# Attention passes of a graph network: bf16 one-hots and their transposes two halves ahead, evicted ahead of the exponential

## The reference, cut to what matters

```python
msg = feat @ W
scores = leaky_relu((msg @ a[:dh])[src] + (msg @ a[dh:])[dst], 0.2)
e = exp(scores - scores.max())
denom = segment_sum(e, dst)
out = segment_sum(msg[src] * (e / denom[dst])[:, None], dst)
```

## Time and profile before

| what | value |
|---|---|
| median of 3 runs | 7888.87 us (7878.3 to 7893.55) |
| span of the profiled execution | 7890.3 us, 195306 instructions |
| its own device time | not listed apart from the span; the span is 1.4 us above the median |
| TensorE matmuls busy | 5464.8 us (69%) |
| VectorE busy | 4825.2 us (61%) |
| ScalarE busy | 3085.2 us (39%) |
| GpSimd busy | 5124.5 us (65%) |
| mean granted TensorE clock | 0.709 |

### The profile page before, as it was taken

How to read it: one execution, slowest core, us unless ns; L and a number is a source line. 1 busy time by engine, 2 the same in 40 slices (tenths; PEclk the granted TensorE clock), 3 DMA queues, 4 the chain that set the end, 5 groups by cost and what they waited for, 6 DMA issues and landing times.

```text
span 7890.3 us, 195306 instructions
## 1 busy us (share of the span) xinstructions
PE 5464.8 (69%) x50500; PEld 3952.8 (50%) x50501; DVE 4825.2 (61%) x14588; ACT 3085.2 (39%) x7615; POOL 5124.5 (65%) x4726
## 2 busy tenths in 40 slices
PE   3767677777773746777776777435878874888887
PEld 3655556565651336666666666323444442444444
DVE  7555555555556556666666666575666663555555
ACT  2111111111121135555555555413555552666665
POOL 1776767676740157777777777025887784777777
PEclk9977675656555855555555555567999996999999
DMA  3223232323233532222222222033555553544444
GB/s 122 57 56 77 56 77 56 77 56 77 56 76 125 148 47 52 52 51 51 51 51 51 51 51 51 12 91 95 124 124 125 124 125 92 120 116 118 118 118 107
DMA packets 600102, 647.29 MB, mean 82 GB/s; under 512 B 331121, under 2 KB 490355, under 8 KB 599665
## 3 DMA queue, kind: packets, MB, share of 16 engines
q0 software_dynamic: 190000, 384.58, 23.9%
q1 hardware_dynamic: 338379, 238.04, 10.4%
q10 hardware_dynamic: 71640, 23.81, 1.2%
HBM read 562.39 MB, written 83.23 MB: 82 GB/s over the span
## 4 chain that ended last, share of the span: by engine, by line
DVE 27%; issue 19%; POOL 15%; DMA 14%; PE 13%; DVEq 5%; ACT 3%; SPq 3%; ACTq 1%; POOLq 0%
POOL acc L659 8%; POOL rows L639 7%; DMA acc<-list_dst 7%; PE psa L1407 4%; PE psc L1366 3%; DMA rows<-t_gat,idx 2%; DVE acc L1729 2%; DVE acc L1781 1%; DMA acc<-in_x 1%; DVEq L619 1%; DMA acc<-y_d 1%; DVE acc L1728 1%; ACT ohb L1120 1%; PE psc L1498 1%; DVE s_m L1837 1%
## 5 line engine op out<-in xcount | busy, mean ns | idle before, releaser
L639 POOL DMA_INDIRECT rows<-t_gat,idx x3168 | 3142.8, 992 | 1189.8 <-issue 903.3
L659 POOL DMA_INDIRECT acc<-t_part,acc x1400 | 1826.6, 1305 | 546.6 <-issue 460.2
L1407 PE MATMUL psa<-rhs,rows 128*128 128x176 f32 (+1 forms) x6336 | 1713.1, 431 | 23.2 <-DVEq L1922 12.2
L1217 ACT ACTIVATE acc<-psa 128x384 bf16<-128x384 f32 x3200 | 1290.2, 506 | 884.7 <-PE psa L1481 765.8
L1407 PEld LDWEIGHTS psa<-rhs,rows 128*128 128x128 f32 x6336 | 1497.2, 311 | 132.0 <-DVEq L1922 83.2
L1481 PE MATMUL psa<-den,rhs 125*32 125x384 bf16 x12800 | 785.2, 343 | 191.4 <-ACT acc L1217 149.8
L1128 ACT ACTIVATE wgt<-s_d 128x64 f32<-128x64 f32 (+1 forms) x396 | 93.8, 237 | 1625.5 <-DVE s_d L1838 1610.8
L1122 ACT ACTIVATE oht<-psc 22x1024 bf16<-22x1024 bf16 x402 | 407.3, 1013 | 783.9 <-PE psc L1366 730.4
L1395 PE MATMUL psc<-oh,wgt 128*8 128x22 f32 (+1 forms) x6336 | 290.2, 205 | 552.1 <-ACT wgt L1128 543.8
L1071 ACT ACTIVATE acc<-stg,acc 128x128 bf16<-128x128 f32 x1818 | 552.9, 387 | 198.2 <-issue 116.0
L1481 PEld LDWEIGHTS psa<-den,rhs 125*32 125x32 bf16 x12800 | 285.6, 97 | 641.9 <-ACT acc L1217 412.7
(11 more groups left out here) (348 smaller groups left out, 7870.4 us busy)
## 6 DMA issues: line engine op xcount, KB each, us to landing
rows<-list_src SPq DMA_DIRECT2D x200, 500.0 KB
rows<-t_gat,idx POOLq DMA_INDIRECT x3168
acc<-y_d SPq DMA_DIRECT2D x50, 1000.0 KB, 5.0
y_d<-stg SPq DMA_DIRECT2D x100, 250.0 KB, 2.8
acc<-t_part,acc POOLq DMA_INDIRECT x1400
acc<-t_sage SPq DMA_DIRECT2D x300, 62.5 KB
adw<-win_d SPq DMA_DIRECT2D x820, 2.2 KB
adw<-win_d SPq DMA_DIRECT2D x788, 0.4 KB
```

What stands on the lines that cost most here:

```text
L639: eng.indirect_dma_start(rows[:, j, 0:spec["width"]], None, spec["table"], bass.IndirectOffsetOnAxis(ap=idx[:, j:j + 1], axis=0)).then_inc ...
L659: eng.indirect_dma_start(h_prow[u][:, t, :], None, t_parts[layer], bass.IndirectOffsetOnAxis(ap=h_idx[u][:, t:t + 1], axis=0)).then_inc(h_ ...
L1217: eng.activation(h_rows[:, g, :], psa[:, g % 4, 0:D3], ACT.Copy).then_inc(hyb["ev"], 1)
L1407: last = eng.matmul(sums(half, q, h), rows[:, slot * TH + j, 0:D], right, start=(j == 2 * q), stop=(j == 2 * q + 1))
```

## The change

It applies to the weighted passes G0 and G1.
- A new order `two_ahead` on TensorE and VectorE: `early` runs two halves ahead, `late` one half ahead. For TensorE `early` is the transposes and `late` the scores; for VectorE `early` is `cur`, `rel` and `ohb`, and `late` is `oh`.
- In G1 VectorE makes `ohb` itself, from `rel_all`; ScalarE's copy L1120 is gone.
- On TensorE the denominators of m are followed at once by pairs 0 and 1; then come the scores of m+1, the transposes of m+2, and pairs 2 and 3.
- On ScalarE `oht` of m+1 is evicted ahead of the exponential of m, and the list work follows the exponential at once.
- `rel` has two buffers. At the end of each run ScalarE evicts once more and TensorE waits for it and increments `adx_ready`; the counters of SP, TensorE and VectorE are moved to suit.

```diff
+        def two_ahead(eng, spec, lo, hi, nxt, early, late, main):
+            slots = spec["slots"]
+            early(lo, 0, True)
+            late(lo, 0, True)
+            early(lo, 1, False)
+            with eng.Fori(lo, hi, spec["step"]) as b:
+                for slot in range(slots - 2):
+                    main(b, slot, lambda: late(b, slot + 1, False), lambda: early(b, slot + 2, False))
+                ahead = next_trip(eng, spec, nxt, b)
+                main(b, slots - 2, lambda: late(b, slots - 1, False), lambda: early(ahead, 0, False))
+                main(b, slots - 1, lambda: late(ahead, 0, False), lambda: early(ahead, 1, False))
...
@@ ScalarE: act_pass
-            def front(b, slot, first):
-                half = slot % 2
+            def evict_oht(b, slot, first):
                 f = count(eng, nf, MAX_HALVES)
-                if h == 1:
-                    eng.wait_ge(oh_ready, f)
-                    eng.activation(ohb[:, half, :, :], oh[:, half, :, :], ACT.Copy).then_inc(ohb_ready, 1)
                 eng.wait_ge(oht_ps, f)
                 eng.activation(oht[:, :, :], p_oht[0:WIN, :, 0:EP], ACT.Copy).then_inc(oht_sb, 1)
+            def run(s0, v, lo, hi, w0):
+                halves(eng, spec, lo, hi, nxt, evict_oht, main)
+                evict_oht(hi, 1, False)
...
                 m = count(eng, nm, MAX_HALVES)
+                next_oht()
                 eng.wait_ge(exp_arg, m)
                 eng.activation(wgt[:, half, :, 0:h], s_d[:, :, 0:h], ACT.Exp).then_inc(wgt_ready, 1)
-                next_front()
@@ TensorE: pe_pass, main and run
-                next_front()
+                if not spec["weighted"]:
+                    next_scores()
                 for q in range(PAIRS):
                     if q == PAIRS // 2 and spec["weighted"]:
-                        scores(1 - half)
+                        next_scores()
+                        next_transposes()
...
+                two_ahead(eng, spec, lo, hi, nxt, transposes, scores_of, main)
+                eng.wait_ge(oht_sb, value(eng, nf))
+                eng.sem_inc(adx_ready, 1)
@@ VectorE: dve_pass
+                def late(b, slot, first):
+                    eng.tensor_tensor(oh[:, slot % 2, :, :], iota_w[:, :].unsqueeze(1).to_broadcast([EP, TH, WIN]),
+                                      rel_of(b, slot).unsqueeze(2).to_broadcast([EP, TH, WIN]),
+                                      ALU.is_equal).then_inc(oh_ready, 1)
+                def early(b, slot, first):
...
+                    if not lists:
+                        shifts(b, slot, link)
+                    if weighted:
+                        eng.tensor_tensor(ohb[:, half, :, :], iota_w[:, :].unsqueeze(1).to_broadcast([EP, TH, WIN]),
+                                          rel_of(b, slot).unsqueeze(2).to_broadcast([EP, TH, WIN]),
+                                          ALU.is_equal).then_inc(ohb_ready, 1)
+                    link.end()
...
-                        eng.wait_ge(adx_ready, value(eng, nf) + 2)
+                        eng.wait_ge(adx_ready, value(eng, nf) + 1)
...
-                    next_front()
+                    next_late()
+                    next_early()
```

More of the change, by code:

```diff
@@ L215, in gnn_kernel @@
         cur = sb("cur", [EP, PAIRS])
-        rel = sb("rel", [EP, TH])
+        rel = sb("rel", [EP, 2, TH])
         oh = sb("oh", [EP, 2, TH, WIN])
@@ L866, in run @@
                 halves(eng, spec, lo, hi, nxt[0], front, main)
+                if spec["weighted"]:
+                    eng.reg_add(nf, nf, 1)
             def after(s):
@@ L1113, in act_pass, with main @@
                 squares, evict, store_idx, counted = act_lists(eng, lists)
-            def front(b, slot, first):
-                half = slot % 2
+            def evict_oht(b, slot, first):
                 f = count(eng, nf, MAX_HALVES)
-                if h == 1:
-                    eng.wait_ge(oh_ready, f)
-                    eng.activation(ohb[:, half, :, :], oh[:, half, :, :], ACT.Copy).then_inc(ohb_ready, 1)
                 eng.wait_ge(oht_ps, f)
                 eng.activation(oht[:, :, :], p_oht[0:WIN, :, 0:EP], ACT.Copy).then_inc(oht_sb, 1)
-            def main(b, slot, next_front):
+            def run(s0, v, lo, hi, w0):
+                halves(eng, spec, lo, hi, nxt, evict_oht, main)
+                evict_oht(hi, 1, False)
+            def main(b, slot, next_oht):
                 half, blk = slot % 2, block_of(spec, b, slot)
                 m = count(eng, nm, MAX_HALVES)
+                next_oht()
                 eng.wait_ge(exp_arg, m)
                 eng.activation(wgt[:, half, :, 0:h], s_d[:, :, 0:h], ACT.Exp).then_inc(wgt_ready, 1)
-                next_front()
                 if lists and half == 0:
@@ L1143, in after @@
                     eng.activation(stg[:, u, :], psa[:, u, 0:CH], ACT.Copy).then_inc(fl_sb, 1)
-            node_ranges(eng, spec, lambda s0, v, lo, hi, w0: halves(eng, spec, lo, hi, nxt, front, main), after)
+            node_ranges(eng, spec, run, after)
             if lists:
@@ L1358, in front, with transposes @@
             def front(b, slot, first):
+                count(eng, nf, MAX_HALVES)
+            def transposes(b, slot, first):
                 half = slot % 2
                 count(eng, nf, MAX_HALVES)
-                if not spec["weighted"]:
-                    return
                 eng.wait_ge(ohb_ready, value(eng, nf))
@@ L1367, in front, with scores_of @@
                 last.then_inc(oht_ps, 1)
-                if first:
-                    scores(half)
+            def scores_of(b, slot, first):
+                scores(slot % 2)
             def scores(half):
@@ L1380, in scores, with main @@
                 last.then_inc(adx_ready, 1)
-            def main(b, slot, next_front):
+            def main(b, slot, next_scores, next_transposes=None):
                 half = slot % 2
@@ L1436, in run @@
                     eng.matmul(sums(1, q, h), zeros[:, :], ones[:, 0:h * WIN], start=True, stop=True).then_inc(sums_ps, 1)
-                halves(eng, spec, lo, hi, nxt, front, main)
+                if not spec["weighted"]:
+                    halves(eng, spec, lo, hi, nxt, front, main)
+                    return
+                two_ahead(eng, spec, lo, hi, nxt, transposes, scores_of, main)
+                eng.wait_ge(oht_sb, value(eng, nf))
+                eng.sem_inc(adx_ready, 1)
             node_ranges(eng, spec, run, after)
@@ L1796, in front, with rel_of @@
                 def front(b, slot, first):
+                    early(b, slot, first)
+                    late(b, slot, first)
+                def rel_of(b, slot):
+                    return rel_all[:, ds(tile_at(spec, b, slot), TH)] if lists else rel[:, slot % 2, :]
+                def late(b, slot, first):
+                    eng.tensor_tensor(oh[:, slot % 2, :, :], iota_w[:, :].unsqueeze(1).to_broadcast([EP, TH, WIN]),
+                                      rel_of(b, slot).unsqueeze(2).to_broadcast([EP, TH, WIN]),
+                                      ALU.is_equal).then_inc(oh_ready, 1)
@@ L1805, in front @@
                     link = DynLinks(eng, dve_w, nl)
-                    if first and weighted:
+                    if first and weighted and not lists:
                         eng.wait_ge(adx_ready, f + 1)
+                    if not lists:
[4 more added lines that the diff above has]
+                                          ALU.is_equal).then_inc(ohb_ready, 1)
@@ L1808, in front, with shifts @@
+                    link.end()
+                def shifts(b, slot, link):
                     link(eng.tensor_scalar(cur[:, :], basef_v[:, base_at(b, slot)], roff[:, 0:1], s1col[:, 0:1],
                                            ALU.add, ALU.min))
-                    link(eng.tensor_tensor(pairs(rel[:, :]), pairs(dstf[:, ds(tile_at(spec, b, slot), TH)]),
+                    link(eng.tensor_tensor(pairs(rel[:, slot % 2, :]), pairs(dstf[:, ds(tile_at(spec, b, slot), TH)]),
                                            cur[:, :].unsqueeze(2).to_broadcast([EP, PAIRS, 2]), ALU.subtract))
[L1812 to L1821, removed]
+                def main(b, slot, next_late, next_early=None):
                     half = slot % 2
@@ L1933, in run @@
                     link.end()
-                halves(eng, spec, lo, hi, nxt, front, main)
+                if weighted:
+                    two_ahead(eng, spec, lo, hi, nxt, early, late, main)
+                    eng.sem_inc(oh_ready, 1)
+                else:
+                    halves(eng, spec, lo, hi, nxt, front, main)
                 add_sums(1)
```

## The result

The changed kernel takes 7775.93 us (median of 4 runs, 7756.0 to 7783.9) where the kernel before, run beside it, takes 7884.42 us (4 runs, 7878.3 to 7893.55): ratio 0.985, 95% interval 0.9837 to 0.9863.

A forecast was written before the change was run, and what follows sets the result against it. Gathers bound the first pass, VectorE's chain with its ScalarE waits the second, gathers close behind. Profiled 7890.3 - 67 (second pass) + 2 (first pass) = 7825, so 7824 us as median; range 7787 to 7864.

The forecast's parts named there:

- both waits at ScalarE: Second pass, VectorE idle at L1768 and L1728: 1.29 to fall to 0.50 us, 0.91 to 0.39 us.
- gather lock: Second pass: one gather each half starts just behind a long VectorE instruction and loses 0.83 us; 7913 us, chance 0.06.
- the chain's term: Second pass, VectorE's program in order: 0.355 us less a half, 10.87 to 10.52 us, 69 us over 195 halves.
- least I see: Second pass, smallest VectorE idle seen between two such stages, 0.39 us, taken as what remains at L1728.
- edits at nothing: Edits counted as 0 us: second buffer of `rel`, moved counters, S0 and S1 passes, SP's DMAs.
- the gathers' limit: Second pass, GpSimd: gathers' own pace of 10.56 us a half puts the last `pen` at about 4900.
- rival B: Second pass: gathers keep 10.2 us, chain cheaper, 10.35 to 10.42 us a half; 7798 us or some 15 lower, chance 0.11.
- D: Second pass: gathers locked onto a long VectorE instruction, 11.03 us a half, 22 us later; 7913 us, chance 0.06.
- Rival A: Second pass: `ohb` hits a gather in every half, 10.73 us a half, gain 37 us less 2; 7854 us, chance 0.18.
- +2 us: First pass: +3 us at range ends, -1.6 us at range starts, sum 2 us longer, bounds -5 and +10.
- L1750's margin: Second pass, odd halves: TensorE's lead at L1750 shrinks from 0.92 to about 0.1 us; up to 20 us if lost.
- The lead of the gathers shrinking over the pass: Second pass, expected sign: gathers' lead shrinks and `pen` waits for rows towards the end.

The follow-up runs named there:

- Experiment 3: The changed kernel with VectorE's half counter put back ahead of `oh` in the second pass, as in the old kernel; 7766.63 us in one run.
- kernel 4: The changed kernel, but VectorE no longer waits for the running maximum before going on to `oh`, in both passes; 7829.7 us (ratio 0.9916).
- Kernel 2: The change in the second pass alone, the first pass keeping the order of the kernel before; 7779.42 us (ratio 0.9854).

## Why the prediction was wrong

**Right: the place and the sign.** The gain is in the second pass, both waits at ScalarE went, the first pass kept its pace, and no gather lock made it slower. L1768's successor idles 0.58 us (0.50 forecast), `ohb` costs 0.25 us (0.30).

**Wrong, the chain's term.** It was "Per even half 0.79 - 0.30 = 0.49, per odd half 0.52 - 0.30 = 0.22; the mean is 0.355". Measured are 0.62 us. The two waits themselves gave 0.73 and 0.55 us where 0.79 and 0.52 were forecast, which all but cancels. (L1728's successor fell to 0.31 us, below the "least I see" of 0.39: that row was idle time at the start of a half, and no floor for this one.) The step that failed is the idle time ahead of `oh`, 0.42 us in the earlier trace rows. It was not in the sum at all, and the moved counters stood among the "edits at nothing"; it gave 0.21 us a half, by far the largest error. Experiment 3 puts 0.08 us of it down to the counter; the cause of the rest is open. By (0.73 + 0.55)/2 + 0.21 - 0.25 the term is 0.60. Over 195 halves the missing 0.265 us is 52 us.

**Wrong, the gathers' limit.** "Their own pace gives: 2827.75 + 196 x 10.56 = 4897.5" took a measured mean for a property of the queue. 10.56 was 9.98 us of bare gathers and what they lost in VectorE's instructions while in step with a chain of 10.87. With the chain at 10.25 us they fell in step at 10.25. The 10.2 us that rivals B and D took from the first pass for an unhindered half was no bare pace either; that is 9.98. The two errors agreed by luck: the chain gave a last `pen` at 4902, the gathers 4900, so either alone would have kept the forecast near 4904, where 4846.5 was measured. Had the gathers' limit been real, the better chain would have brought nothing. This second error is why rival B, which had the direction right, got only 0.11 ("10.2 never held in this pass"). The range's lower end was B's chain at 10.34, and the measured chain at 10.25 went 18 us below that. Rival A's and D's mechanism is real, and kernel 4 shows it, but it costs time only where the rows are late; here the lead stays at 9 to 10 gathers.

**Small terms.** First pass "+2 us": the start of the second pass came 2.96 us sooner, inside the bounds and inside what the variants differ by. Kernel 2 gives its value as nil within 0.15%. L1750's margin held, with more to spare than forecast: 0.67 us are left of 0.92, not 0.1. "The lead of the gathers shrinking over the pass, and `pen` waiting for rows towards its end" did not come.

The rule of the Trainium skill ("SBUF — State Buffer", section "Who interferes with whom": a VectorE instruction with two SBUF inputs contends with GpSimd's reads) spoke against the move. The traces agree with the rule, down to one-hots of 0.34 us, but not with that use of it: in the changed kernel no gather of the second pass starts inside `ohb` (L1845), so it costs the gathers nothing. In kernel 4, at other phases, 123 do, with a mean of 1.025 us. The gathers' mean between 3500 and 4500 even fell, from 1.020 to 0.977 us, with one such instruction more in each half. (The 17.4 us put down to `psa` in the second row are the usual 0.30 us, 57 times.)

```profile
L639 POOL DMA_INDIRECT rows<-t_gat,idx x737 | 751.8, 1020 | 248.8 <-issue 187.1 <-PE psa L1407 61.7
```

```profile
L652 POOL DMA_INDIRECT rows<-t_gat,idx x781 | 762.8, 977 | 238.0 <-issue 220.6 <-PE psa L1427 17.4
```

## What to carry to other kernels

Where two engines run beside each other without waiting and one lengthens the other's instructions, the measured pace of the lengthened one is no limit of its own: take its bare time as the lower bound, and ask at which phase it will settle. Then sum the idle gaps of the whole chain by line and not just those with a foreign releaser, since register work that moves out of a gap can be a gain as well. And a chain made shorter than the feeding queue can be slower than a longer one; look whether the consumer's waits for data appear.

## What the runs showed of the hardware

- Gathers fall in step with VectorE without any semaphore: with chains of 10.25, 10.32 and 10.64 us a half, their lengthening settled at 0.26, 0.33 and 0.65 us, each time within 0.02 us of the chain less the bare 9.98.
- What is seen to hold a gather up is a TENSOR_TENSOR on VectorE with both inputs in SBUF, whatever the type. In the second pass of the nine traces at the usual time 2639 gathers start at least 0.05 us into one with at least 0.16 us of it left: 2124 times all bf16, 515 times a one-hot or `rhs` with f32. Every one ends 0.81 to 0.83 us behind the instruction. The 351 that start between 0.06 us ahead of one of the long ones and 0.03 us into it take 0.94 to 0.95 us. So do the 850 that start in the 1.35 us TENSOR_REDUCE.
- Three of them in the rows shown: 0.19 us into the 1.36 us L1741 of kernel 4, ended 3417.53 - 3416.71 = 0.82 us behind it; 0.07 us into the 1.02 us L1781 of the earlier trace rows, 3728.93 - 3728.11 = 0.82 us behind that; 0.06 us into the 0.34 us f32 `oh` of the earlier trace rows, 3723.48 - 3722.65 = 0.83 us behind that. One that started 0.04 us ahead of L1741 took 0.94 us.
- The kernel before took 7878 to 7918 us in four sets of runs and 9164 to 9333 us in four others, where all variants' medians lay within 0.6% of it. Two chips stand on both sides.
